# The edge update's normalisation, moved from rows to columns through a shared PSUM bank

## The reference

```python
h = relu(LN(x))
em = relu(LN([h[src], h[dst]] @ msg_w + msg_b) * msg_g + msg_beta) * edge_weight
messages = segment_sum(em, dst) / counts          # zero where a node has no edge
gate = sigmoid(h @ gate_w + gate_b)
u = relu(LN([h, messages] @ upd_w + upd_b) * upd_g + upd_beta)
out = x + gate * u + (1 - gate) * h
```

## Time and profile before

| | |
|---|---|
| median of 3 runs | 885.0 us (884.76 to 885.63) |
| profiled execution | 884.2 us, span 882.5 us |
| busy: PE, DVE, ACT, POOL | 671.8, 839.0, 827.3, 621.3 us |
| mean granted PE clock | 0.932 |

### The profile page before, as it was taken

How to read it: one execution, slowest core, us unless ns; L and a number is a source line. 1 busy time by engine, 2 the same in 40 slices (tenths; PEclk the granted TensorE clock), 3 DMA queues, 4 the chain that set the end, 5 groups by cost and what they waited for, 6 DMA issues and landing times.

```text
span 882.5 us, 20426 instructions
## 1 busy us (share of the span) xinstructions
PE 671.8 (76%) x4448; PEld 524.5 (59%) x4448; DVE 839.0 (95%) x3820; ACT 827.3 (94%) x3476; POOL 621.3 (70%) x602
## 2 busy tenths in 40 slices
PE   1888888888788888876677878787887877777871
PEld 1655555555555555554566767676666766666760
DVE  6899999999999999999988999999999999999893
ACT  2899999999999999998899999999999999999972
POOL 4777777777777777777577777666666657655377
PEclk9999999999999999998789899889899899998985
DMA  5355665666565566653132232332212111211110
GB/s 154 93 175 183 179 180 178 179 196 196 182 205 190 195 200 188 197 190 116 57 106 80 73 108 85 102 96 93 70 58 70 58 66 59 69 63 48 55 66 33
DMA packets 60437, 107.96 MB, mean 122 GB/s; under 512 B 14567, under 2 KB 16439, under 8 KB 60371
## 3 DMA queue, kind: packets, MB, share of 16 engines
q1 hardware_dynamic: 39756, 71.88, 24.4%
q0 software_dynamic: 18912, 34.84, 13.9%
q10 hardware_dynamic: 1702, 0.53, 0.3%
HBM read 56.01 MB, written 55.12 MB: 126 GB/s over the span
## 4 chain that ended last, share of the span: by engine, by line
ACT 78%; issue 9%; DVE 5%; POOL 3%; PE 2%; ACTq 1%; DMA 1%; POOLq 0%
ACT hrow L395 22%; ACT junk L402 21%; ACT work L1070 8%; ACT xload L395 7%; ACT work L433 6%; ACT lnv L377 4%; POOL out L607 3%; ACT at L1070 2%; ACT work L1127 2%; ACT work L1125 2%; ACT rs L382 1%; ACT work L1075 1%; DVE st L353 1%; DMA shift_col<-in_L_gnn_upd_beta 1%; ACTq L113 1%
## 5 line engine op out<-in xcount | busy, mean ns | idle before, releaser
L607 POOL DMA_INDIRECT out<-work,sidx x196 | 202.5, 1033 | 122.5 <-issue 56.5
L602 POOL DMA_INDIRECT ring<-in_x,src_i x196 | 210.2, 1072 | 72.1 <-issue 57.6
L395 ACT ACTIVATE hrow<-xload,nb,rs 128x128 f32<-128x128 f32 x392 | 208.4, 980 | 1.3 <-DVE nb L388 1.3
L402 ACT ACTIVATE junk<-py 128x128 bf16<-128x128 f32 x588 | 198.3, 589 | 4.4 <-PE py L1246 3.6
L402 ACT ACTIVATION_READ_ACCUMULATOR junk<-py 128x1 f32 x588 | 184.9, 523 | 0.0
L602 POOL DMA_INDIRECT ring<-in_x,gidx x140 | 148.5, 1061 | 46.1 <-issue 41.7
L1075 ACT ACTIVATE work<-pa,shift_col,gain_col 128x512 f32<-128x512 f32 x94 | 119.2, 1268 | 0.0
L1246 PE MATMUL py<-w_u,work 128*128 128x129 f32 x784 | 116.4, 293 | 0.0
L1204 PE MATMUL pt<-ident,hrow 128*128 128x128 f32 x588 | 102.5, 300 | 10.5 <-ACT hrow L395 10.2
L1246 PEld LDWEIGHTS py<-w_u,work 128*128 128x128 f32 x784 | 97.3, 195 | 21.8 <-issue 21.8
L1070 ACT ACTIVATE work<-pt 128x512 f32<-128x512 f32 (+1 forms) x99 | 106.5, 1076 | 3.0 <-PE pt L1204 3.0
(11 more groups left out here) (170 smaller groups left out, 1956.4 us busy)
## 6 DMA issues: line engine op xcount, KB each, us to landing
xload<-in_x SPq DMA_DIRECT2D x98, 256.0 KB, 3.4
out<-work SPq DMA_DIRECT2D x98, 256.0 KB
running_sums<-acc SPq DMA_DIRECT2D x49, 256.0 KB, 2.1
staged_target_rows<-work SPq DMA_DIRECT2D x14, 256.0 KB, 3.2
ring<-staged_target_rows SPq DMA_DIRECT2D x14, 256.0 KB, 3.2
ring<-in_x,src_i POOLq DMA_INDIRECT x196
out<-work,sidx POOLq DMA_INDIRECT x196, 2.2
ring<-in_x,gidx POOLq DMA_INDIRECT x140, 3.0
```

The costliest lines, as they stand in the source:

```text
L395: last = nc.scalar.activation(dest[:, m, :], rows[:, m, :], ACT.Relu, bias=nb[:, s4, at + m:at + m + 1], scale=rs[:, s4, at + m:at + m + 1])
L402: last = nc.scalar.activation(junk[:, j, k, :], prod[:, k, 0:H], ACT.Square, scale=scale, accum_out=mv[:, slot, at + k, 1:2])
L602: pool.indirect_dma_start(out=dest, out_offset=None, in_=rows, in_offset=bass.IndirectOffsetOnAxis(ap=idx, axis=0), **(if_tail if rows is ...
L607: pool.indirect_dma_start(out=out, out_offset=bass.IndirectOffsetOnAxis(ap=idx, axis=0), in_=rows, in_offset=None, **if_tail).then_inc(s, 16)
```

## The change

For all edge groups, `gamma` becomes one 128x512 multiplication by rstd (`scaled`); PE transposes its result into `pa` (`turned`, after the message matmuls); ACT rectifies it there with gamma as scale and beta as bias, both one value per partition (`turned_relu`); PE transposes the result back into the same `pa` (`back`, its last part of the step); and DVE multiplies by the gate and adds to the mixed row, four 128x128 instructions (`gated_sum`, for s-8, after the statistics of the source rows). `beta`, the gated relu and `final` fall away for edges. Since `pa` is now shared, `aflip` of s-5 waits for the gated sum of s-8 (mark `final`), and `turned` of s-7 for the copy `at` of s-5. On ACT, `post` comes ahead of the copy `at`. PE's steps run to EG + 7 instead of EG + 5. In the node stage two pieces of code become functions, with the same instructions. The diff, without those pieces and some context:

```diff
@@ -46,6 +46,7 @@
 TURNED = NG - 4
 J = 196
 EG = J // G
+TURNED_EDGES = EG
 EPAD = P * J
 FULL = E // J
 REST = E - FULL * J
...
@@ -421,9 +422,13 @@
                 L.wait()
                 L.mark(nc.scalar.activation(gt[:, b, :], e1[:, b, :], ACT.Exp, scale=-1.0))
 
+        def turned_edges(g):
+
+            return g.at < TURNED_EDGES
+
         def shifted(d, g):
 
-            return g.back(TURNED) if d is nd else g
+            return g.back(TURNED) if d is nd else g.back(TURNED_EDGES) if d is ed else g
 
         def gated_relu(act, d, g, n=G, first=0, done=True):
 
@@ -473,6 +478,21 @@
         def beta(dve, d, g, t, by, n=G):
             d["gamma"].after(dve, g)
             one_mark(d["beta"], dve, shifted(d, g), nc.vector.tensor_tensor(t, t, over_rows(by, n), ALU.add))
+
+        def scaled(dve, d, g, slot, at):
+
+            one_mark(d["gamma"], dve, g, nc.vector.tensor_tensor(
+                t_buf[:, g.at % 4], py[:, g.at % 2, :, 0:H],
+                rs[:, slot, at:at + G].unsqueeze(2).to_broadcast([P, G, H]), ALU.mult))
+
+        def gated_sum(dve, d, f, prod):
+
+            d["mix"].after(dve, f)
+            d["back"].after(dve, f)
+            for k in range(G):
+                last = nc.vector.scalar_tensor_tensor(o[:, f.at % 4, k, :], prod[:, k, :], gt[:, f.at % 4, k:k + 1],
+                                                      o[:, f.at % 4, k, :], ALU.mult, ALU.add)
+            one_mark(d["final"], dve, f, last)
 
         def final(eng, vec, d, g, dest, n=G):
             d["mix"].after(eng, g)
...
@@ -908,7 +921,7 @@
                 if s.at == EG:
                     early = mix_early(2)
                 f = s.back(8)
-                if live(f, EG):
+                if live(f, EG) and not turned_edges(f):
                     final(dve, nc.vector, ed, f, o[:, f.at % 4])
                 if drained and s.at <= EG + 2:
                     early = mix_early(early + 1)
@@ -916,6 +929,8 @@
                     dve.wait_ge(s_gsrc[s.at % 4], s.rounds(G * 16, G * 16))
                     L = ed["stats"]
                     row_stats(L, s, slot(s, 0), 0)
+                if live(f, EG) and turned_edges(f):
+                    gated_sum(dve, ed, f, rows4(pa[:, :]))
                 if live(s.back(1), EG):
                     minus_mean(dve, ed, s.back(1), 2 * G, -0.5)
                 q = s.back(3)
@@ -928,8 +943,11 @@
                     node_rows(node)
                 if fin:
                     ed["rstd"].after(dve, s)
-                    one_mark(ed["gamma"], dve, g, by_std(t_buf[:, g.at % 4], py[:, g.at % 2], s.at % 4, 3 * G, g_upd))
-                    beta(dve, ed, g, t_buf[:, g.at % 4], be_upd)
+                    if turned_edges(g):
+                        scaled(dve, ed, g, s.at % 4, 3 * G)
+                    else:
+                        one_mark(ed["gamma"], dve, g, by_std(t_buf[:, g.at % 4], py[:, g.at % 2], s.at % 4, 3 * G, g_upd))
+                        beta(dve, ed, g, t_buf[:, g.at % 4], be_upd)
                 if new:
                     L.begin(dve, s)
                     if s.at >= DIRECT:
@@ -1069,11 +1087,11 @@
                 d[flip].after(act, g)
                 one_mark(d[stage], act, g, nc.scalar.activation(dest, source, func))
 
-            def turned_relu(r):
-
-                nd["turned"].after(act, r)
-                one_mark(nd["relu"], act, r, nc.scalar.activation(
-                    t_buf[:, r.at % 4].rearrange("p k h -> p (k h)"), pa[:, :], ACT.Relu, bias=shift_col[:, :],
+            def turned_relu(d, r, source):
+
+                d["turned"].after(act, r)
+                one_mark(d["relu"], act, r, nc.scalar.activation(
+                    t_buf[:, r.at % 4].rearrange("p k h -> p (k h)"), source, ACT.Relu, bias=shift_col[:, :],
                     scale=gain_col[:, :]))
 
             def node_step(s):
...
@@ -1130,14 +1148,14 @@
                     if live(n, NG):
                         evacuate(nd, n, ht_dst[:, n.at % 4, :], pt[:, n.at % 2, :], ACT.Copy, "ht", "flip")
                     if turned(node.back(5)):
-                        turned_relu(node.back(5))
+                        turned_relu(nd, node.back(5), pa[:, :])
                     if not turned(node.back(6)):
                         gated_relu(act, nd, node.back(6))
+                if live(s.back(6), EG):
+                    post(act, ed, s.back(6), (s.at + 1) % 4, 3 * G, G, 1.0)
                 g = s.back(5)
                 if live(g, EG):
                     evacuate(ed, g, at_[:, g.at % 2, :], pa[:, :], ACT.Copy, "at", "aflip")
-                if live(s.back(6), EG):
-                    post(act, ed, s.back(6), (s.at + 1) % 4, 3 * G, G, 1.0)
                 g = s.back(1)
                 if live(g, EG):
                     ed["nb"].after(act, g)
@@ -1155,8 +1173,11 @@
                 if live(s.back(6), EG):
                     gates(act, s.back(6), 1)
                 if live(s.back(7), EG):
-                    ed["gate"].after(act, s.back(7))
-                    gated_relu(act, ed, s.back(7))
+                    if turned_edges(s.back(7)):
+                        turned_relu(ed, s.back(7), pa[:, :])
+                    else:
+                        ed["gate"].after(act, s.back(7))
+                        gated_relu(act, ed, s.back(7))
                 if live(s.back(2), EG):
                     ed["msg"].after(act, s.back(2))
                     one_mark(ed["square_m"], act, s.back(2), squares(pm, (s.at + 1) % 4, 2 * G, G, 1, 1.0))
@@ -1255,6 +1276,8 @@
                 g = s.back(5)
                 if live(g, EG):
                     ed["sum"].after(pe, g)
+                    if beyond(g, 3) and turned_edges(g.back(3)):
+                        ed["final"].after(pe, g.back(3))
                     one_mark(ed["aflip"], pe, g, flip(pa[:, :], acc[:, g.at % 4]))
                 g = s.back(2)
                 if live(g, EG):
@@ -1271,6 +1294,14 @@
                         last = nc.tensor.matmul(pm[:, k, :], ht_dst[:, (g.at + NG) % 4, k * H:(k + 1) * H], w_all[:, 1, :],
                                                 start=False, stop=k == G - 1)
                     one_mark(ed["msg"], pe, g, last)
+                g = s.back(7)
+                if live(g, EG) and turned_edges(g):
+                    ed["gamma"].after(pe, g)
+                    if live(s.back(5), EG):
+                        ed["at"].after(pe, s.back(5))
+                    elif beyond(g, 1):
+                        ed["final"].after(pe, g.back(1))
+                    one_mark(ed["turned"], pe, g, flip(pa[:, :], t_buf[:, g.at % 4]))
                 g = s.back(1)
                 if live(g, EG):
                     ed["h"].after(pe, g, 1)
@@ -1296,6 +1327,10 @@
                     ed["flip"].begin(pe, g)
                     ed["flip"].n = 1
                     ed["flip"].mark(flip(pt[:, 1, :], h_dst[:, (g.at + NG) % XS]))
+                g = s.back(7)
+                if live(g, EG) and turned_edges(g):
+                    ed["relu"].after(pe, g)
+                    one_mark(ed["back"], pe, g, flip(pa[:, :], t_buf[:, g.at % 4]))
 
             node_step(Group(0))
             node_step(Group(1))
@@ -1305,7 +1340,7 @@
             pe.wait_ge(s_b3, 16)
             pe.wait_ge(s_prep, WEIGHTS)
             run_steps(pe, node_step, NG, 2, 9, 8, first=2, beside=edge_step)
-            straight_steps(edge_step, EG, 5, 2)
+            straight_steps(edge_step, EG, 7, 2)
 
 
             z = Group(0)
```

More of the change, by code:

```diff
@@ L326, in build @@
         tl.update(stages("tail", {"msg": 1, "sum": 1, "aflip": 1, "at": 1}))
-        ed = stages("edge", {**common, "stats": 4, "h": 2, "ht": 1, "flip": 2,
+        ed = stages("edge", {**common, "turned": 1, "back": 1, "stats": 4, "h": 2, "ht": 1, "flip": 2,
                              "gamma_m": 1,
@@ L731, in node_rows @@
                     if turned(g):
-                        one_mark(nd["gamma"], dve, g, nc.vector.tensor_tensor(
-                            t_buf[:, g.at % 4], py[:, g.at % 2, :, 0:H],
-                            rs[:, s.at % 4, G:2 * G].unsqueeze(2).to_broadcast([P, G, H]), ALU.mult))
+                        scaled(dve, nd, g, s.at % 4, G)
                     else:
@@ L750, in node_sum @@
                 if live(f, NG) and turned(f):
[L751 to L756, removed]
+                    gated_sum(dve, nd, f, pm)
                 elif live(f, NG):
@@ L1085, in node_step @@
                 if live(s.back(5), NG):
-                    turned_relu(s.back(5))
+                    turned_relu(nd, s.back(5), pa[:, :])
                 rstds(act, nd, s, 2 * G)
```

## The result

| | before | after |
|---|---|---|
| median | 885.32 us (884.76 to 887.11) | 960.39 us (957.41 to 961.17) |
| ratio, 95% interval | | 1.0838 (1.0810 to 1.0866) |
| profiled execution, span | 884.2, 882.5 us | 960.84, 958.7 us |
| busy: PE, DVE, ACT, POOL | 671.8, 839.0, 827.3, 621.3 us | 748.1, 798.6, 817.8, 634.8 us |
| mean granted PE clock | 0.932 | 0.910 |

A forecast was written before the change was run, and what follows sets the result against it. ACT bounded the kernel at 8.63 us a step; the change would close a PE-DVE loop of 8.79, 9.93 with slow steps. 41 x 1.30 = 53 us plus 1 for the drain on 885.0 gave 939 us, range 888 to 958.

The forecast's parts named there:

- the 2.48 of the sum: Edge-step loop, end of `back` through gated sum, nb and `gamma_m` to PE's message matmuls: 2.48 us.
- 6.31: Edge-step loop on PE, message matmuls through `turned`, hrow, update and h_dst to the end of `back`: 6.31 us.
- the bounds of 8.70 to 9.2: Full-clock edge step, taken as 8.79 us: 8.70 with a shorter last hand-over, 9.2 with every transpose set at 0.59.
- The price of a slow step: PE's slow clock in an edge step: 1.7 us more than at full clock.
- I take two steps of three: Share of looped edge steps with PE's slow clock: two of three, making the mean step 9.93 us.
- I take 1: Drain after the loop, group 41 to the end: 54.4 us again, with 1 us added for the clock.
- the 5.8: Drain steps of edge groups 44 to 46: 5.8 us each.
- up to 3 more if the clock falls there: Drain: upper allowance of 3 us over 54.4 should PE's clock fall.
- Only the engines and the bank: Rival for the edge loop: ACT's 8.15 us step rules, 20 us less, 865 us; chance 0.06.
- Full clock: Rival for the edge loop: no slow steps, 8 us more, 893 us; chance 0.20.
- Every step falls: Rival for the edge loop: every step slow, 79 us more, 964 us; chance 0.18.
- The signs: Edge stage: gated sum and messages wait, ACT idles 0.7 to 2 us, steps about 8.8 and 10.4, clock under 0.9.

The follow-up runs named there:

- e2: Changed kernel with PE transposing the running sums twice into `pa`, four more transposes a step: 922.57 us, 1.0430 of the kernel before.
- e7: Changed kernel with PE transposing the running sums three times, eight more transposes a step: 914.98 us, 1.0338 of the kernel before.
- e10: Changed kernel, steps 8 to 47: gated sum after `gamma_m`, `aflip` after messages, half the target rows, `at`, then squares on ACT; last nine groups old way: 863.54 us.
- e5: Changed kernel, gated sum after `gamma_m`, `aflip`, hrow, `turned` after messages; on ACT half the target rows and squares ahead of `at`: 964.23 us, 1.0890.
- e1: Changed kernel with DVE's gated sum moved behind `gamma_m` instead of ahead of nb: 937.05 us, 1.0584 of the kernel before.
- e3: Kernel before the change with the running sums transposed three times into `pa`, eight more transposes a step: 885.67 us, 1.0013.
- e6: Changed kernel, gated sum after `gamma_m`, `aflip`, hrow, `turned` after messages; on ACT squares, then `at`, ahead of all target rows: 886.77 us, 1.0019.

## Why the prediction was right in its direction and wrong in its size

The mechanism held. The loop from `back` over the gated sum, nb, `gamma_m` and the messages to `back` again is in the rows: `back` ends at 657.10, the gated sum starts at 657.21, the messages at 659.59, 2.49 us against the 2.48 of the sum. From the messages to the end of `back` are 6.40 at full clock (650.70 to 657.10) against 6.31; the 0.09 is the flip of hrow, 0.54 to the next start (653.32 to 653.86), which I had priced at 0.44 like a set inside a stream. The step is 8.89 and not 8.79, within the bounds of 8.70 to 9.2: 41 x 0.10 = 4 us of the miss.

The price of a slow step was right: 1.63 (10.53 - 8.90) for 1.7; 2 us less in all. One reading of the kernel before was not in its rows: of the two waits of DVE for ACT in each step, the waits from 480 to 820 us there list 8 of nb for rstd, 1.5 us in all, and none of the final sum. Nothing in the sum hangs on it.

**The failed step is the share: "I take two steps of three".** It is 33 of 41, in runs of four or five with one full step behind each: (0.80 - 0.67) x 41 x 1.7 = 9 us. I had argued it by the nearness of the gap's idle time to the 2.07 us waits that fell before, and had seen that nothing keeps a slow step from following a slow one; for the share itself, between the every second step of the kernel before and every step, the prediction has no working. Rows of after bear out that the gap does not shrink: it is 1.38 and 0.48 us after a full step and after a slow one (658.48, 669.02), and slow steps come in series. Where a series ends, the trace shows too. Three narrow windows (columns as above) and the start of the messages in the last slow step of the series shown:

```profile
660.50:661.00 0.50, 0.50 (x5) 0.50 (x5) 0.50 (x3) 0.50 (x3) 0.21 (x1) 0.70 0.00 0
681.00:681.50 0.50, 0.50 (x4) 0.50 (x4) 0.50 (x4) 0.50 (x3) 0.50 (x1) 0.68 0.27 97
701.50:702.00 0.50, 0.32 (x1) 0.10 (x1) 0.50 (x2) 0.50 (x2) 0.20 (x1) 0.66 0.00 0
```

```profile
701.68 0.58 PE L1231 MATMUL pm<-bias,ones 3*128 3x512 bf16 x1 [0.48 <-DVE acc L470]
```

From their means, at levels 1.00 and 0.50, the clock falls at 660.70, 681.18 and 701.66. These are two steps apart each, so the falls of this series follow each other by 10.24 us while its steps are some 10.5 long. Each fall comes nearer to the start of the messages: 1.11 us behind it in the first slow step (659.59), none in the fifth. The next fall at that spacing would have come at 711.9, inside PE's gap; there is none, and that step is the full one. The other six series of the loop end in the same way; why no fall comes in the gap is open, and so is why 13 of 41 are left in e2. That the gap is what brings the slow steps, e2 and e7 show, though not whether by its shorter idle time or by the work put into it; e10, which adds no work and idles 1.07 us a step instead of 1.86, speaks for the idle time, though its step is shorter too.

**The second mis-sized term, as large as the first, is the drain: "I take 1".** It is 11.6. Groups 42 and 43 came after 10.53 and 9.59 instead of 8.8 and 7.9, and 44 to 46 after 7.99, 9.03 and 7.83 instead of 5.8 each; from there 21.0 us remain, against 20. In e2 and e7 the steps of 44 to 46 take 6.62 and 7.06 at a clock of 1.00 with 0.43 and 0.87 of transposes added, so 6.2 without: the 5.8 was 0.4 short at full clock. The other 1.6 to 2.8 a step is put down to the clock; e5 bears it out, with 6.18 and 6.19 at a clock of 1.00 for groups 44 and 45 and 9.03 at 0.65 for 46. The windows of the steps that end with the gated sums of 44 and 45 (columns as above):

```profile
912.86:920.85 7.99, 5.67 (x30) 4.84 (x30) 5.61 (x19) 3.36 (x18) 4.63 (x4) 0.79 0.16 56
920.85:929.90 9.05, 6.84 (x30) 5.52 (x30) 3.92 (x15) 4.12 (x22) 3.93 (x4) 0.65 0.14 49
```

The clock is 0.79 and 0.65, below the 0.87 of the loop, with PE idle for 2.2 to 2.3 us in each. I had allowed "up to 3 more if the clock falls there", and had then applied the forecast's clock to the loop and not to the drain. Together: 4 - 2 + 9 of the loop and 10.6 of the drain, some 22 us.

The rivals. *Only the engines and the bank*: not this kernel, but its price of ACT's step, 8.15, is what e10 measures, 8.10. The turns in the bank cost nothing by themselves here: e10 makes the same six a step and its step is ACT's own. They are what the Trainium skill asks for (PSUM — Partial Sum Buffer, section "PSUM bank collisions raise a hardware error": accesses of two engines kept apart by semaphores, by bank); what breaking the rule would do, no run here shows. *Full clock*: refuted by the clock of 0.87; e7 comes nearest, with no slow step. *Every step falls* gave 964 and came closest in time, by luck, as two errors cancel: eight steps did not fall, and the drain was dearer. With a slow step and the drain as measured it would be 885 + 41 x 1.90 + 12 = 975.

The signs: gated sum and messages wait in each of 39 steps; ACT idles (7 us in 40, 1.8 a step); two lengths, 8.89 and 10.53; the clock 0.87, under 0.9. All as said. But 0.88 was the clock for two in three, so the clock could not tell the share; the intervals do.

## What to carry to other kernels

When a change threads work back and forth between engines that run in a written order, follow the queues once around: a step cannot be shorter than any closed loop over one step, and cutting the longest loop only shows the next (e1, e5), so list them all before moving a line. An engine that comes onto such a loop brings its idle gaps and its clock with it, also into the drain; where the same gap recurs in every step, price a slow stretch in all of them as the bound (33 of 41 here), and not by how often it fell while the engine had slack. The instructions that cost 75 us in one order gain 22 in another (e10, its last groups in the old way), so a change of the work and the order it is put in are two things to measure.

## What the runs showed of the hardware

- More work on PE made the kernel faster: four transposes a step in its idle gap gave back 38 us (e2: 20 fewer slow steps of 1.63 us, and 7 us of the drain), eight 45 us (e7). These are fp32 transposes through the identity, and with eight the clock of the window from 640 to 680 us is 1.00 (e7, e3), where it was 0.87 and 0.91.
- Two gaps of 1.38 and 0.48 us with one set of transposes between them were followed by the 1.2 GHz level in 33 of 41 steps, in the step shown 1.1 us into the message matmuls (660.70). With the second gap all but filled (e2, one of 1.38 left) it was 13 of 41; with a gap of 1.80 us for `at` (e5) 28 of 41. In e6 and e10, with gaps of 1.05 and 0.25 and of 0.63 and 0.44, it is 1.00 from 480 to 840 and from 480 to 800 us.
